# Embedding all eight image pairs in the first stage of a ViT block, before the attention steps

## What is computed

```python
h = conv_16x16_stride_16(x) + conv_b + pos_table[ids]        # 16 images, 49 tokens, 192 wide
h = h + attention(layernorm(h))                              # 12 heads of 64, causal mask, softmax
h = h + moe(layernorm(h))                                    # 8 experts, top 2, capacity 245, hidden 512
```

## Time and profile before

| | |
|---|---|
| median of 3 runs | 260.85 us (259.34 to 261.6) |
| span of the profiled execution, first to last instruction | 258.2 us |
| its device time beside the span | not given |
| mean granted TensorE clock of the core | 0.893 |
| busy: PE, DVE, ACT, POOL | 193.2, 135.7, 105.5, 102.4 us |
| head, until the first `soften` | 0 to 33.6 us |
| steps −2 to 2, until `queries_keys(1)` | 33.6 to 68.5 us |
| bytes moved by DMA | 24.72 MB |

### The profile page before, as it was taken

How to read it: one execution, slowest core, us unless ns; L and a number is a source line. 1 busy time by engine, 2 the same in 40 slices (tenths; PEclk the granted TensorE clock), 3 DMA queues, 4 the chain that set the end, 5 groups by cost and what they waited for, 6 DMA issues and landing times. The chain is left out here.

```text
span 258.2 us, 4448 instructions
## 1 busy us (share of the span) xinstructions
PE 193.2 (75%) x1508; PEld 171.6 (66%) x1508; DVE 135.7 (53%) x391; ACT 105.5 (41%) x231; POOL 102.4 (40%) x117
## 2 busy tenths in 40 slices
PE   5969999898999797788669499999868689430000
PEld 1948998788998696687433399999768679430000
DVE  6487467686826788886676136555434452000000
ACT  1146733546463657347262236665334442101000
POOL 9330033333231445765669000718061707244270
PEclk9999999999999999979967779999979799875555
DMA  7977405303010000110110272586747223120212
GB/s 204 410 272 240 134 3 168 159 3 118 7 36 3 1 26 13 36 38 22 35 37 17 70 280 110 208 212 192 213 129 166 60 33 71 14 25 7 30 9 22
DMA packets 18801, 24.72 MB, mean 96 GB/s; under 512 B 10142, under 2 KB 14507, under 8 KB 17632
## 3 DMA queue, kind: packets, MB, share of 16 engines
q1 hardware_dynamic: 6896, 21.50, 24.0%
q0 software_dynamic: 11520, 2.63, 8.0%
q10 hardware_dynamic: 368, 0.36, 0.5%
HBM read 21.26 MB, written 5.15 MB: 102 GB/s over the span
## 5 line engine op out<-in xcount | busy, mean ns | idle before, releaser
L800 POOL DMA_INDIRECT out<-qT,toke x16 | 39.7, 2480 | 69.5 <-issue 42.2
L523 PE MATMUL ps<-xp,v 128*123 128x192 f32 x128 | 23.7, 341 | 3.4 <-ACT qT L694 3.4
L512 PE MATMUL ps<-zeA,wqkv 128*128 128x246 f32 x64 | 19.5, 305 | 8.6 <-DVE zeR L1029 8.6
L765 POOL DMA_INDIRECT slots<-row,slot x16 | 20.6, 1290 | 10.4 <-issue 4.6
L523 PEld LDWEIGHTS ps<-xp,v 128*123 128x123 f32 x128 | 22.0, 197 | 3.7 <-issue 3.7
L1034 DVE TENSOR_TENSOR v<-v,ps 128x246 f32<-128x246 f32 x32 | 12.6, 407 | 20.7 <-ACT v L686 20.6
L757 POOL TENSOR_TENSOR sm<-sm,smax 128x588 f32<-128x588 f32 x8 | 10.6, 1328 | 27.9 <-DVE smax L865 27.6
L1018 DVE TENSOR_TENSOR wqkv<-raw,wqkv 128x1024 fp32r<-128x1024 f32 x16 | 19.3, 1221 | 3.9 <-ACT wqkv L674 3.7
L441 PE MATMUL ps<-filler 128*128 128x512 bf16 x64 | 19.8, 468 | 1.3 <-POOL filler L723 1.3
L686 ACT ACTIVATE v<-ps 128x246 f32<-128x246 f32 x32 | 12.0, 376 | 20.9 <-PE ps L514 20.8
L508 PE MATMUL ps<-zeA,wqkv 128*128 128x246 f32 x64 | 20.0, 313 | 0.0
(11 more groups left out here) (141 smaller groups left out, 537.3 us busy)
## 6 DMA issues: line engine op xcount, KB each, us to landing
raw<-w SPq DMA_DIRECT2D x8, 1025.0 KB, 5.8
xp<-w SPq DMA_DIRECT2D x8, 384.0 KB, 5.0
xp<-patches SPq DMA_DIRECT2D x8, 294.0 KB, 6.1
raw<-w_qkv SPq DMA_DIRECT2D x3, 768.0 KB, 9.2
slots<-blank SPq DMA_DIRECT2D x8, 196.0 KB, 3.8
xp<-slots SPq DMA_DIRECT2D x8, 196.0 KB, 5.4
out<-base SPq DMA_DIRECT2D x8, 73.5 KB
convw<-conv_w SPq DMA_DIRECT2D x2, 288.0 KB, 4.9
```

The lines of the kernel that those rows point to most:

```text
L512: mm(o, wsp[:, j, 0, 0, w], zeA[:, j, 1, :], start=False, stop=False)
L523: last = mm(ps[0:EROWS, 6 + r, 0:D], hT[:, j, jt, r * EROWS:(r + 1) * EROWS], w2s[:, j, jt, :], start=(jt == 0), stop=(jt == JT - 1))
L765: P.indirect_dma_start(slots, bass.IndirectOffsetOnAxis(slot[:, p % PH, k:k + 1], 0), row[:, p % 2, k, :], None, bounds_check=EXPERTS * ST ...
L800: P.indirect_dma_start(out, bass.IndirectOffsetOnAxis(toke[:, j, r:r + 1], 0), ye[0:EROWS, j, r, :], None, bounds_check=N + STRIDE - 1, oo ...
```

## The change

All eight pairs' patches are loaded and embedded in the head. `xp`, `y`, `yA` and `yR` get a place for every pair, SP issues the second four loads between those of `w_qkv` and without a wait, PE does the four later convs where the filler stood, and the transposes, `y_hi` and `y_lo` of pairs 4 to 7 stand between `queries_keys(0)` and the first step. `embedded` goes.

```diff
-        xp = sb("xp", [128, PH, KC, PT])
+        xp = sb("xp", [128, PAIRS, KC, PT])
-        y = sb("y", [PT, 2, D])
-        yA = sb("yA", [128, 2, PH, 128], f32r)
-        yR = sb("yR", [128, PH, 128], f32r)
+        y = sb("y", [PT, PAIRS, D])
+        yA = sb("yA", [128, 2, PAIRS, 128], f32r)
+        yR = sb("yR", [128, PAIRS, 128], f32r)
...
         def conv_bank(p):
-            return PH + p if p < PH else 6
+            return PH + p % PH
         def yt_bank(p):
-            return p if p < PH else 7 if p < PAIRS - 2 else p % 2
+            return p if p < PH else (2, 3, 6, 7)[p - PH]
...
# SP
-            for w in range(3):
-                sp.dma_start(raw[:, w * 2 * QKV:(w + 1) * 2 * QKV], w_qkv[w]).then_inc(ld_qkv[w], 16)
+            sp.dma_start(raw[:, 0:2 * QKV], w_qkv[0]).then_inc(ld_qkv[0], 16)
+            for p in LAST[0:2]:
+                sp.dma_start(xp[:, p], patches[p]).then_inc(ld_x[p], 16)
+            sp.dma_start(raw[:, 2 * QKV:4 * QKV], w_qkv[1]).then_inc(ld_qkv[1], 16)
+            for p in LAST[2:]:
+                sp.dma_start(xp[:, p], patches[p]).then_inc(ld_x[p], 16)
+            sp.dma_start(raw[:, 4 * QKV:6 * QKV], w_qkv[2]).then_inc(ld_qkv[2], 16)
-            for p in FIRST:
-                sp.wait_ge(conv_done, p + 1)
-                sp.dma_start(xp[:, p], patches[PH + p]).then_inc(ld_x[p], 16)
...
# PE, conv: a pair of the second half reuses the bank of pair p - 4
-                    pe.wait_ge(h_ready, p)
-                if p == PAIRS - 1:
-                    pe.wait_ge(h2_ready, 1)
+                    pe.wait_ge(h_ready, p - PH + 1)
# PE, transpose_y
-                if p == PH:
-                    pe.wait_ge(h_ready, PH)
-                    pe.wait_ge(bo_ready, 1)
-                elif p == PH + 1:
-                    pe.wait_ge(ylo_ready, p)
-                elif p > PH:
-                    pe.wait_ge(sm_ready, PH)
+                if PH <= p < PH + 2:
+                    pe.wait_ge(ylo_ready, p - 1)
+                elif p >= PH + 2:
+                    pe.wait_ge(h_ready, p + 1)
# PE, values
+                if p == 0:
+                    pe.wait_ge(ylo_ready, PH + 2)
# PE, queries_keys
+                    if not half and n == 2:
+                        pe.wait_ge(h_ready, PH + 2)
# PE, project
-                pe.wait_ge(h_ready, PAIRS - 1 if p == 0 else PAIRS)
                 if p == 0:
+                    pe.wait_ge(ylo_ready, PAIRS)
# PE, transpose_y2
-                pe.wait_ge(ylo_ready, PH + 2)
+                if p == 0:
+                    pe.wait_ge(bo_ready, 1)
# PE, bias_values
-                pe.wait_ge(h_ready, PH)
+                pe.wait_ge(ylo_ready, PAIRS)
# PE, order
-            keep_busy(8, conv_bank(0))
+            for p in LAST[0:2]:
+                conv(p)
             transpose_y(PH - 1)
-            keep_busy(6, conv_bank(0))
+            for p in LAST[2:]:
+                conv(p)
             pe.wait_ge(all_zeroed, 1)
             queries_keys(0)
+            for p in LAST:
+                transpose_y(p)
...
-                if s in (0, 1, 2):
-                    transpose_y(PH + s)
-                if s == PH - 2:
-                    transpose_y(PAIRS - 1)
-                for p in embedded(s):
-                    conv(p)
# ACT, order
             queries_keys(0, range(HP, 2 * HP))
+            for p in LAST:
+                y_hi(p)
-                if s in (0, 1, 2):
-                    y_hi(PH + s)
-                if s == PH - 2:
-                    y_hi(PAIRS - 1)
# POOL, order
-            for p in FIRST:
+            for p in range(PAIRS):
                 norm(p)
-                for p in embedded(s - 1):
-                    norm(p)
# DVE, norm
-                if p >= 2:
-                    dve.wait_ge(yt_done, p - 1)
# DVE, order, behind y_lo(3)
-            for w in (1, 2):
-                for c in range(2):
-                    split_qkv(w, c)
+            embed(4)
+            split_qkv(1, 0)
+            norm(4)
+            embed(5)
+            split_qkv(1, 1)
+            norm(5)
+            embed(6)
+            embed(7)
+            norm(6)
+            norm(7)
+            for c in range(2):
+                split_qkv(2, c)
...
             keys(0, range(HP))
+            for p in LAST:
+                y_lo(p)
-                for p in embedded(s - 1):
-                    norm(p)
-                if s in (0, 1, 2):
-                    y_lo(PH + s)
-                if s == PH - 2:
-                    y_lo(PAIRS - 1)
-                for p in embedded(s):
-                    embed(p)
```

More of the change, by code:

```diff
@@ L157, in vit_block @@
         ld_conv = [sem(f"ld_conv{j}") for j in range(2)]
-        ld_x = [sem(f"ld_x{p}") for p in range(PH)]
+        ld_x = [sem(f"ld_x{p}") for p in range(PAIRS)]
         ld_qkv = [sem(f"ld_qkv{w}") for w in range(3)]
@@ L212, in in_pairs @@
             return 0 <= p < PAIRS
-        def embedded(s):
-            return (s + PH + 2,) if -2 <= s < 2 else ()
         @block.sync
@@ L292, in conv @@
             def conv(p):
-                pe.wait_ge(ld_x[p % PH], 16 * (1 + p // PH))
+                pe.wait_ge(ld_x[p], 16)
                 if p >= PH:
-                    pe.wait_ge(h_ready, p)
-                if p == PAIRS - 1:
-                    pe.wait_ge(h2_ready, 1)
+                    pe.wait_ge(h_ready, p - PH + 1)
                 for c in range(KC):
@@ L300, in conv @@
                         pe.wait_ge(ld_conv[c // CA], 16)
-                    last = mm(ps[0:PT, conv_bank(p), 0:D], xp[:, p % PH, c, :], convw[:, c, :], start=(c == 0), stop=(c == KC - 1))
+                    last = mm(ps[0:PT, conv_bank(p), 0:D], xp[:, p, c, :], convw[:, c, :], start=(c == 0), stop=(c == KC - 1))
                 last.then_inc(conv_done, 1)
@@ L306, in transpose_y @@
                 pe.wait_ge(y_ready, p + 1)
-                if p == PH:
-                    pe.wait_ge(h_ready, PH)
-                    pe.wait_ge(bo_ready, 1)
-                elif p == PH + 1:
-                    pe.wait_ge(ylo_ready, p)
-                elif p > PH:
-                    pe.wait_ge(sm_ready, PH)
-                nc.tensor.transpose(ps[:, bank, 0:PT], y[:, p % 2, 0:DA], ident[0:PT, 0:PT])
-                nc.tensor.transpose(ps[0:DR, bank, 128:128 + PT], y[:, p % 2, DA:D], ident[0:PT, 0:PT]).then_inc(yt_done, 1)
+                if PH <= p < PH + 2:
+                    pe.wait_ge(ylo_ready, p - 1)
+                elif p >= PH + 2:
+                    pe.wait_ge(h_ready, p + 1)
+                nc.tensor.transpose(ps[:, bank, 0:PT], y[:, p, 0:DA], ident[0:PT, 0:PT])
+                nc.tensor.transpose(ps[0:DR, bank, 128:128 + PT], y[:, p, DA:D], ident[0:PT, 0:PT]).then_inc(yt_done, 1)
             def values(p):
@@ L320, in values @@
                 pe.wait_ge(ylo_ready, p + 1)
+                if p == 0:
+                    pe.wait_ge(ylo_ready, PH + 2)
                 if p >= 1:
                     pe.wait_ge(pt_ready, p)
-                q = p % PH
+                q = p
                 for j in range(2):
@@ L352, in tokens @@
                     def tokens(t):
-                        return t.rearrange("p a (i s) -> p (a i) s", i=2)[:, :, 0:EVEN]
+                        return t[:, PH * half:PH * (half + 1)].rearrange("p a (i s) -> p (a i) s", i=2)[:, :, 0:EVEN]
                     mm(o, wqkv[:, w, 0, 0, c], tokens(yA[:, 0]), start=True, stop=False)
@@ L552, in y_hi @@
                 act.wait_ge(yt_done, p + 1)
-                q, bank = p % PH, yt_bank(p)
+                q, bank = p, yt_bank(p)
                 A(yA[:, 0, q, :].rearrange("q (i s) -> q i s", i=2)[:, :, 0:TOK], ps[:, bank, 0:PT].rearrange("q (i t) -> q i t", i=2), ACT.Copy)
@@ L831, in norm @@
                 dve.wait_ge(rstd_ready, p + 1)
-                if p >= 2:
-                    dve.wait_ge(yt_done, p - 1)
-                V.tensor_scalar(y[:, p % 2, :], h[:, p, :], mv[:, p % 2, 0:1], rstd[:, p % 2:p % 2 + 1], ALU.subtract, ALU.mult).then_inc(y_ready, 1)
+                V.tensor_scalar(y[:, p, :], h[:, p, :], mv[:, p % 2, 0:1], rstd[:, p % 2:p % 2 + 1], ALU.subtract, ALU.mult).then_inc(y_ready, 1)
             def y_lo(p):
                 dve.wait_ge(yhi_ready, p + 1)
-                q, bank = p % PH, yt_bank(p)
+                q, bank = p, yt_bank(p)
                 def two(t):
```

## The result

The first measurement, four executions, gave the changed kernel a median of 263.43 us (262.19 to 265.84) against 261.23 us before: ratio 1.018, 95% interval 1.010 to 1.026. The forecast of 262.0 us was a change of 0.4%, and this says 1.8% (the two medians by themselves stand only 0.84% apart, so four executions carry the ratio weakly). Two later sets of twelve executions each gave 1.0063 (1.0024 to 1.0102) and 1.0022 (0.9981 to 1.0063). Weighted by their intervals the three make 1.0058, give or take 0.0026, which is 1.5 us on 260.85 (0.8 to 2.2). The three differ by more than their intervals allow (the first begins at 1.010, the pooled one ends at 1.0084), so the true error of the pooled figure is larger than that. So the change costs time, but less than the first four runs show, and a good part of the work is to tell what belongs to the change from what belongs to the execution.

What follows compares the result with a forecast made beforehand. Head (0 to 33 us) bounded by DMA, then PE; steps −2 to 2 by a round over four engines. Head +6.1 less steps 4.95 gives +1.15 on the 260.85 median: 262.0 us, range 257.6 to 265.4.

Steps and rivals of the forecast that it cites:

- The head: Up to `soften(0)`: the added convs and late `y_lo` start it at 39.7 instead of 33.58, +6.1 us.
- half 0 to `soften(0)`: From the start of half 0 of `queries_keys` to the first `soften`: 14.7 us predicted.
- The four convs: PE in the head: four convs of 2.11 us replace the fillers, half 0 starts at 25.0 instead of 20.74, +4.3 us.
- The DVE sum: DVE in the head from 22.2: four embeds, four norms and four splits take 9.3 to 9.4 us, until 31.6.
- the key copies caught up: DVE's key copies in half 0: taken as 0 late, bounds 0 to 0.6 us, catching up 0.3 us per key block.
- +1.15: Everything behind half 1 comes later by the head's 6.1 less the steps' 4.95 us.
- The steps: From `soften(0)` to half 1 of `queries_keys`: 29.95 us instead of 34.91, −4.95 us.
- round over four engines: Steps −2 to 2: bounded by DVE, POOL, ACT and PE in turn; the convs there only partly on the path.
- Rival A: PE sets the steps: 9.2 us gained against the head's 6.1, so −3.1 and 257.7 us; chance 0.20.
- rival B: Granted clock falls in the thinned steps: 1.3 us per fall, two falls +2.6, 264.6 us; chance 0.22.
- the list of what would prove me wrong: `soften(0)` before 38, half 1 before 67 (A), or granted clock below 1.00 between 40 and 70 us (B).

Runs made afterwards that it cites:

- short convs in the kernel before: Kernel before, convs of pairs 4 to 7 doing one chunk of six: median 262.87 us, ratio 1.0044 to the kernel before.
- before, more filler at the start: Kernel before with 13 instead of 8 filler matmuls ahead of the first conv: median 260.63 us, ratio 0.9984.
- late `y_lo`: Changed kernel with DVE doing `y_lo` of pairs 4 to 7 behind `soften(0)`: median 261.54 us, ratio 1.0006 to the kernel before.
- short convs: Changed kernel, convs of pairs 4 to 7 doing one chunk of six: median 261.02 us, ratio 1.0016 to the kernel before.
- reordered: Changed kernel with `conv(4)` ahead of `transpose_y(2)`, and late pairs' transposes behind `scores(0)`, their `y_lo` behind `soften(0)`: 260.38 us, ratio 0.9951 to before.
- filler in the pause: Changed kernel with 13 filler matmuls on PE before `values(1)` in step 0: median 262.33 us, ratio 1.0041 to the kernel before.
- reordered, filler in the pause (three kernels): Reordered kernel plus 13 fillers before `values(1)`: 259.19 us (0.9924); also 13 instead of 8 at start: 258.16 (0.988); also six each in steps 3-5: 257.91 (0.9871).

## Why the prediction was wrong, and where it was right

**The head.** Right in its largest part. The table above has half 0 to `soften(0)` as predicted to 0.35 us. The four convs cost nearly what the sum said: half 0 at 23.99 in the second trace, with its first conv 0.5 us earlier than before, is 17.85 behind that conv, against 18.35 predicted and 14.09 before, so +3.8 and not +4.3. In all, `soften(0)` is 32.9 us behind the first conv (39.06 − 6.14) where it was 26.9: +6.0, predicted +6.1. The DVE sum was 1.2 us too small (10.6 for 9.4): I took one wait of 1.06 us for POOL where there are 0.72, 0.72 and 0.53, and missed that POOL is slower beside DVE's split. It cost little only because the key copies caught up, which the prediction had bounded.

**What the sum took as unchanged.** I counted from a first conv at 6.65 us, and in all ten traces of the changed kernel and its variants it starts at 6.06 to 6.37, against 6.55 to 6.79 in the three of the kernel before. And the time of an execution beside its span, which I took as the same, is 1.8 us in the executions of the changed kernels (1.75 to 1.92) and 2.2 in those of the kernel before and its variants (2.13 to 2.29). What makes these two differences is open. With them the work that was moved costs next to nothing: without a fall and without the slow first convs, half 1 stands at 68.75 (the trace with the filler) for 68.49, +0.3 us where I had +1.15, and −0.1 us with the time beside the span.

**The steps.** Right. Without a fall, `soften(0)` to half 1 takes 29.69 us, in the trace with the filler (39.06 to 68.75) and in the third trace of the changed kernel (41.00 to 70.69). Predicted were 29.95. The reading of the steps as a round over four engines was tested by the short convs in the kernel before: what PE did there between `soften(0)` and `soften(2)` was not on the path. **Rival A** is refuted by the same run.

**The step that failed is the granted clock, which the forecast put at nothing.** I set the fall aside as rival B, at 0.22, and gave the likeliest case none, although its sign (a clock below 1.00 between 40 and 70 us) was on the list of what would prove me wrong. The pause was as I had it, 3.15 us measured for 3.2. The granted clock below is read over 50 to 56 us, where not marked.

| trace | PE's pause before `values(1)` | granted clock | `soften(2)` to `zs(0)` | `soften(0)` to half 1 |
|---|---|---|---|---|
| before | 1.45 | 1.00 | 4.24 | 34.91 |
| before, more filler at the start | 1.46 | 1.00 | 4.25 | 34.90 |
| before, short convs | 2.70 | 0.72 (47 to 53) | 4.53 | 36.37 |
| after, first trace | 3.15 | 0.61 (50 to 58) | 6.37 | 32.14 |
| after, second | 3.14 | 0.72 | 5.32 | 31.06 |
| after, third | 3.15 | 1.00 | 4.18 | 29.69 |
| late `y_lo` | 3.15 | 0.77 | 5.26 | 31.25 |
| short convs | 2.43 | 0.77 | 5.35 | 31.09 |
| reordered | 3.16 | 0.77 | 5.39 | 31.50 |
| filler in the pause | filled | 1.00 | 4.19 | 29.69 |
| reordered, filler in the pause (three kernels) | filled | 1.00 | 4.19 to 4.20 | 30.05 to 30.06 |

Five of the six traces that left the pause show the fall, the four with the filler in it none, and the kernel before shows none until its own pause grows to 2.70 us. In these five the price at `zs(0)` was 1.1 to 1.2 us four times and 2.2 in the one with the longer fall, against my 1.3 each and 2.6 for two; by half 1 it is 1.4 (31.06 − 29.69). One fall, not two, is the rule. The argument against it (a pause of 1.45 us that cost nothing) compared a pause with one twice as long.

So the cost of the change has another make-up than the forecast: about nothing from the moved work, where I had +1.15, and 1.4 us from one fall, where I had none. The three measurements together say +1.5 (0.8 to 2.2), and the filler in the pause is worth 1.0 (0.2 to 1.7) of it. That the later medians (262.5 and 262.1) lie so near the forecast of 262.0 is luck: one term was too large by nearly what the other left out. The sum doesn't close everywhere either: with the filler in the pause the kernel should be level with the one before, and its ratio is 1.0041 (1.0004 to 1.0078); what the slower eight of its executions lose is open.

**The first measurement said +1.8%** (its medians +0.84%) and the later ones 0.6% and 0.2%. The one trace that goes with it has besides the fall in step 0, there longer than in any other trace, a slow start of the first convs (+1.45), which comes in kernels old and new, and the fall at 92 us. A second trace of the changed kernel has this fall too, at 89 us, and the reordered kernel at 87; the third trace of the changed kernel has not. Whether it is tied to the change is open: it is also in the trace of the kernel before with more filler at its start, at 88 us. The other three executions of the first measurement have no trace, so what made them slow is not shown.

The Trainium skill (TensorE: Matmul & The Clock Gate, "Why this matters for your kernels") warns that an idle gap between bursts of matmuls puts the array back to its lower clock. The traces agree in most cases: behind the pause of 3.15 us the clock fell, and cost 2.1 us in the first trace. In the third trace the same pause passed without a fall, and pauses of 2.43 and 2.70 us (the two kernels with the short convs) had one behind them.

## What to carry to other kernels

Work that fills an engine's unavoidable pauses costs little; pulled forward to where that engine is the one everybody waits for, the same work costs what is left of it once the pauses and the filler there are used up, here 3.8 us at half 0 for four convs of 2.1. What is won back at the old place is only the part that was on the path there, here 5.2 us of DVE, ACT and waits for 9.2 us of PE. After such a move look at the PE pauses it leaves: put cheap matmuls in a long pause whose end is known, but none that reach past it into the time of an instruction that others wait for. Order the moved work around the first instruction that opens the next stage: three moves, two of which put `scores(0)` and `soften(0)` first, turned a change of +0.6% into −0.5%, and with the fillers −1.2%.

## What was not expected of the hardware

- The first conv matmuls ran at half rate in three of the traces (10 or 11 instructions in 7 to 10 us where 20 or 21 stood), and the profile's granted clock reads 1.00 in that stretch. Whether it was the clock is not shown; for the pace of PE in a head, look at the spacing of equal matmuls and not at that column alone.
- POOL's subtraction of the row maximum takes 2.22 us when DVE's split of `w_o` lies beside it and 1.17 us when the late `y_lo` do (second trace of the changed kernel and the kernel with the late `y_lo`). The same holds for the small `rstd` instruction, 0.80 for 0.19 us. What DVE runs beside POOL matters, not only that it is busy.
- Removing PE work made the kernel before no faster and rather slower (1.0044, 1.0006 to 1.0082); its trace has two falls of the clock, behind PE waits of 2.70 and 2.40 us.
- An execution takes 1.8 us more than its span in the changed kernels and 2.2 us in the kernel before; why is open. A comparison of spans alone would miss 0.4 us in favour of the change.
